# Graph network on one core: head projections of the first layer one round later, and another order of VectorE's products

## The reference

```
msg_s, msg_v = (projected node)[src] + (projected node)[dst]
m1_s, m1_v   = tensor product of msg with y, weighted by rbf @ W_rbf        # "M"
a            = leaky(m1_s @ W_alpha) . alpha_dot                            # logits, "alog"
val_s, val_v = m1_s @ Ws_val, m1_v @ Wv_val ; val_v *= sigmoid(val_s @ Wg)
m2_s, m2_v   = tensor product of (sigmoid(val_s), val_v) with y             # "M2"
h            = m2_s @ Ws_vlin, m2_v @ Wv_vlin                               # head values, "h_tab"
out          = node + (softmax over each destination of a, times h, summed) @ Wp
```

## Time and profile before

| what | value |
|---|---|
| median of three runs | 4853.46 us (4850.1 to 4861.61) |
| span of the profiled execution | 3828.1 us |
| own time of the profiled execution, beyond its span | not given |
| first layer's rounds | from 82 to 2226 us of the span |
| softmax, sums, node work | between the two |
| second layer's products (L1844) | from 2668 to 3766 us |
| TensorE / VectorE / ScalarE / GpSimd busy, of the span | 3407.1 / 3541.0 / 3089.1 / 2570.9 us |

### The profile page before, as it was taken

One profiled execution on the slowest core, in us unless ns is written; L12 is line 12 of the kernel. 1 busy time (PEld: TensorE's weight loads), 2 busy tenths in 40 slices (PEclk: granted clock), 3 DMA queues, 4 the chain that ended last, 5 costly groups with the idle time before them and its releaser, 6 DMA issues. The chain is left out here.

```text
span 3828.1 us, 96308 instructions
## 1 busy us (share of the span) xinstructions
PE 3407.1 (89%) x21340; PEld 2641.0 (69%) x21340; DVE 3541.0 (92%) x12738; ACT 3089.1 (81%) x11217; POOL 2570.9 (67%) x2469
## 2 busy tenths in 40 slices
PE   4899999999999999999999939976999999999997
PEld 3888888888888888888888838864333333333335
DVE  5999999999999999999999978874999999999995
ACT  4888899899989988988899847754787877778774
POOL 1777777777777777777777711111777777777772
PEclk8999999999999999999999979987999999999999
DMA  4333333333333333333333359971333433343333
GB/s 110 89 95 92 92 95 94 92 95 93 95 94 93 95 92 94 93 93 93 94 93 95 93 186 270 274 204 44 92 94 95 95 94 95 95 95 93 95 94 115
DMA packets 299642, 411.02 MB, mean 107 GB/s; under 512 B 98580, under 2 KB 234772, under 8 KB 299316
## 3 DMA queue, kind: packets, MB, share of 16 engines
q0 software_dynamic: 127008, 208.99, 24.2%
q1 hardware_dynamic: 172564, 201.26, 16.3%
HBM read 309.09 MB, written 100.94 MB: 107 GB/s over the span
## 5 line engine op out<-in xcount | busy, mean ns | idle before, releaser
L658 POOL DMA_INDIRECT SC<-dst_tab,idx x784 | 904.5, 1154 | 238.8 <-issue 237.3
L721 POOL DMA_INDIRECT ACC<-hid_tab,idx x784 | 811.4, 1035 | 348.6 <-issue 340.3
L658 POOL DMA_INDIRECT ACC<-src_tab,idx x784 | 758.5, 967 | 313.1 <-issue 164.2
L800 PE MATMUL TR<-ident,M 128*128 128x128 f32 x4704 | 664.4, 277 | 136.9 <-DVE M L1529 135.5
L800 PEld LDWEIGHTS TR<-ident,M 128*128 128x128 f32 x4704 | 520.1, 141 | 229.9 <-DVE M L1529 229.8
L1124 ACT ACTIVATE MT<-TR 128x768 f32<-128x768 f32 x784 | 596.9, 825 | 3.5 <-PE TR L800 3.5
L1113 ACT ACTIVATE ACC<-W,ACC 128x64 f32<-128x64 f32 x2352 | 577.7, 336 | 0.0
L849 PE MATMUL HP<-w_hv,MT 128*128 128x128 f32 x3136 | 520.2, 288 | 0.0
L824 PE MATMUL E<-w_mv,MT 128*128 128x128 f32 x3136 | 476.7, 275 | 0.0
L824 PEld LDWEIGHTS E<-w_mv,MT 128*128 128x128 f32 x3136 | 436.6, 191 | 0.0
L1306 ACT ACTIVATE ACC<-TR,y 128x128 f32<-128x128 f32 (+1 forms) x1568 | 417.2, 551 | 1.3 <-PE TR L982 1.2
(11 more groups left out here) (278 smaller groups left out, 7662.5 us busy)
## 6 DMA issues: line engine op xcount, KB each, us to landing
h_tab<-ACC SPq DMA_DIRECT2D x392, 160.0 KB
SC<-h_tab SPq DMA_DIRECT2D x50, 640.0 KB, 4.8
TAB<-h_tab SPq DMA_DIRECT2D x48, 640.0 KB, 5.2
ACC<-in_e64T SPq DMA_DIRECT2D x98, 256.0 KB
ACC<-src_tab,idx POOLq DMA_INDIRECT x784
SC<-dst_tab,idx POOLq DMA_INDIRECT x784
ACC<-hid_tab,idx POOLq DMA_INDIRECT x784, 3.4
agg_tab<-ACC POOLq DMA_DIRECT2D x49, 240.0 KB, 4.0
```

What stands on the lines that cost most here:

```text
L658: pool.indirect_dma_start(gat[:, v.slot8, g, :], None, table.ap(), bass.IndirectOffsetOnAxis(ap=idx[:, v.sslot, c + g:c + g + 1], axis=0))\
L721: pool.indirect_dma_start(gat1[:, v.slot8, g, :], None, hid_tab.ap(), bass.IndirectOffsetOnAxis(ap=idx[:, v.sslot, c:c + 1], axis=0))\
L800: ins = nc.tensor.transpose(to[:, b * G + g, :], Mt[:, g, lo:lo + w], ident[:, :])
```

## The change

TensorE's stage had e1(t-1), t2(t-2), t1(t), factors0(t+2), hm(t-2). It now has hm(t-3) between t2 and t1. MT2 gets a second buffer and ScalarE's copy into it waits for hm of two rounds before instead of one. `scalars0`, `head_products`, `head_values` and `store` move to round t-3, and the loops of those four engines end one stage later. GpSimd is as before.

VectorE's order becomes, by the old line numbers: 1540, 1478, 1546, 1503, 1554, 1509, 1557, 1567, 1581, 1603, 1583, 1584, 1585, 1591, 1593, 1612, 1514, 1515, 1521, 1522, 1528, 1529. For this `summed` is split into `summed` and `lifted`, `mixed` into `mixed_dots` and `mixed_crosses`, `mixed_sums` into `mixed_dot_sums` and `mixed_cross_sums`, and `sum_of_dots0` is taken out of `rest_of_s0`. Each function keeps the waits of its instructions, and `mixed_dots` has those of `mixed`.

```diff
+        MT2s = (MT2, sb("MT2b", [P, 3, G, P]))
 # SP
-                store(t + -2, total)
-            loop_steps(sp, Q, NS, False, 7, 2, sp0)
+                store(t + -3, total)
+            loop_steps(sp, Q, NS, False, 7, 3, sp0)
 # TensorE (hm reads MT2s[v.par] instead of MT2)
                 t2(t + -2, total)
+                hm(t + -3, total)
                 t1(t, total)
                 factors0(t + 2, total)
-                hm(t + -2, total)
-            loop_steps(pe, Q, NS, False, 2, 2, stage0)
+            loop_steps(pe, Q, NS, False, 2, 3, stage0)
 # ScalarE, copies
-                if v.past(1):
-                    act.wait_ge(LA[freed], v.num)
+                if v.past(back):
+                    act.wait_ge(LA[freed], v.num + 1 - back)
 ...
-                copies(t + -2, total, "t2", TR2, MT2, "c2", "h")
-                copies(t, total, "t1", TR1, MT, "c1", "e1")
+                copies(t + -2, total, "t2", TR2, MT2s[(t + -2).par], "c2", "h", 2)
+                copies(t, total, "t1", TR1, MT, "c1", "e1", 1)
 ...
-                scalars0(t + -2, total)
-            loop_steps(act, Q, NS, False, 2, 2, stage0)
+                scalars0(t + -3, total)
+            loop_steps(act, Q, NS, False, 2, 3, stage0)
 # VectorE, stage0
                 gated(t + -1, total)
                 added = messages(t + 1, total)
                 ups = gated_up(t + -1, total)
-                done = summed(t + -1, total, ups)
                 parts = products0(t + 1, total, added)
+                summed(t + -1, total)
+                crossed0(t + 1, total, parts)
+                done = lifted(t + -1, total, ups)
                 scaled(t + -1, total, done)
-                crossed0(t + 1, total, parts)
-                mixes = mixed(t + -1, total)
-                mixed_sums(t + -1, total, mixes)
-                up = head_products(t + -2, total)
+                dots = mixed_dots(t + -1, total)
+                up = head_products(t + -3, total)
+                crosses2 = mixed_crosses(t + -1, total)
+                mixed_dot_sums(t + -1, total, dots)
+                mixed_cross_sums(t + -1, total, crosses2)
+                head_values(t + -3, total, up)
                 crosses = others0(t + 1, total, parts)
-                head_values(t + -2, total, up)
+                sum_of_dots0(t + 1, total, parts)
                 rest_of_s0(t + 1, total, parts)
                 rest_of_v0(t + 1, total, parts, crosses)
-            loop_steps(dve, Q, NS, False, 1, 2, stage0)
+            loop_steps(dve, Q, NS, False, 1, 3, stage0)
```

More of the change, by code:

```diff
@@ L846, in hm @@
                 for g in range(G):
-                    nc.tensor.matmul(HP[:, S * g:S * (g + 1)], MT2[:, 0, g, :], w_hs0[:, :], start=True, stop=True)
+                    nc.tensor.matmul(HP[:, S * g:S * (g + 1)], MT2s[v.par][:, 0, g, :], w_hs0[:, :], start=True, stop=True)
                     for b in range(2):
-                        ins = nc.tensor.matmul(HP[:, P + P * g:P + P * (g + 1)], MT2[:, 1 + b, g, :], w_hv0[:, b, :],
+                        ins = nc.tensor.matmul(HP[:, P + P * g:P + P * (g + 1)], MT2s[v.par][:, 1 + b, g, :], w_hv0[:, b, :],
                                                start=(b == 0), stop=(b == 1))
@@ L1115, in weigh0, with copies @@
                     ins.then_inc(LA["ws"], 1)
-            def copies(v, total, turned, tr, dst, sem_done, freed):
+            def copies(v, total, turned, tr, dst, sem_done, freed, back):
                 if not inside(v, total):
@@ L1515, in others0, with sum_of_dots0 @@
                     return ch.count(TT(fX[:, :, 2], feat(S + 2 * C, (-2 * C, 2), (1, C)), wgt(192, (128, 2), (1, C)), ALU.mult))
-            def rest_of_s0(v, total, parts):
+            def sum_of_dots0(v, total, parts):
                 if parts:
@@ L1521, in rest_of_s0 @@
                     TT(mid(C, (1, C)), mid(0, (1, C)), mid(C, (1, C)), ALU.add)
+            def rest_of_s0(v, total, parts):
+                if parts:
+                    mid, feat, wgt, dots = parts
                     TT(mid(96, (S, 2), (1, S)), feat(0, (0, 2), (1, S)), wgt(C, (S, 2), (1, S)), ALU.mult)
@@ L1547, in gated_up, with summed @@
                                        ALU.mult))
-            def summed(v, total, up):
+            def summed(v, total):
                 if not inside(v, total):
@@ L1555, in summed, with lifted @@
                                                  ax(la[:, 0, 0:1], (LG, G * H), (1, LG)), AX.X, ALU.add))
+            def lifted(v, total, up):
+                if not inside(v, total):
+                    return
                 ch.wait(up)
@@ L1568, in scaled, with mixed_dots @@
                     .then_inc(LA["vg"], 1)
-            def mixed(v, total):
+            def mixed_dots(v, total):
                 if not inside(v, total):
@@ L1579, in vec, with mixed_crosses, mixed_dot_sums, mixed_cross_sums @@
                     return ax(V2[:, 0, C * k:C * k + 1], (96, G), *dims)
-                dots = ch.count(TT(ax(M2[:, v.par, 0, 0:1], (M0, G), (C, 3), (1, C)), vec(0, (C, 3), (1, C)),
+                return ch.count(TT(ax(M2[:, v.par, 0, 0:1], (M0, G), (C, 3), (1, C)), vec(0, (C, 3), (1, C)),
                                    y_of(v, 1, (1, 3), (0, C)), ALU.mult))
+            def mixed_crosses(v, total):
+                if not inside(v, total):
+                    return
+                def vec(k, *dims):
+                    return ax(V2[:, 0, C * k:C * k + 1], (96, G), *dims)
                 TT(fX2[:, :, 0:2, 0, :], vec(0, (C, 2), (1, C)), y_of(v, 2, (1, 2), (0, C)), ALU.mult)
                 TT(fX2[:, :, 0:2, 1, :], vec(1, (C, 2), (1, C)), y_of(v, 1, (1, 2), (0, C)), ALU.mult)
[L1585 to L1589, removed]
+                return ch.count(TT(fX2[:, :, 2], vec(2, (-2 * C, 2), (1, C)), y_of(v, 1, (2, 2), (0, C)), ALU.mult))
+            def mixed_dot_sums(v, total, dots):
+                if inside(v, total):
                     ch.wait(dots)
                     TT(M2[:, v.par, :, C:2 * C], M2[:, v.par, :, 0:C], M2[:, v.par, :, C:2 * C], ALU.add)
+            def mixed_cross_sums(v, total, crosses):
+                if inside(v, total):
                     ch.wait(crosses)
```

## The result

| comparison | kernel before | changed kernel | ratio, 95% interval |
|---|---|---|---|
| first, the one that was predicted | 4857.5 us | 5055.3 us (5039.3 to 5076.8) | 1.042 [1.039, 1.046] |
| second | 3818.8 us | 3946.1 us | 1.034 [1.032, 1.036] |
| third, on yet another chip | 3818.7 us | 3938.8 us | 1.031 [1.030, 1.033] |

The change makes the kernel slower in all three comparisons, by 198 us in the first comparison and by 127 and 120 us later. The forecast was +96 us and 4949 us, in a range up to 4990. The time is outside the range.

What follows compares the result with a forecast made beforehand. VectorE and GpSimd were taken to run at the same pace, 5.455 us a round. VectorE's 5.32 + 0.34 for pairs + 0.04 left of delays gave 5.70, +96 us over 390 rounds: 4949 us, range 4888 to 4990 (ends +41, +135).

Steps and rivals of the forecast that it cites:

- e1: TensorE's matmuls after ScalarE's copy of TR1; forecast to start 1.75 us after t1, ending near 4.0, over 1 us before `gated`.
- The base: Level the loss was added to: 5.455 us rounds from a 3828.1 us span, 1025 us around it unchanged.
- The pairs: VectorE's dependent neighbours: lifted to scaled (first) costs 0.22, scaled to mixed_dots (second) 0.12, together 0.34 us a round.
- The rule on the semaphore that costs nothing: Between two VectorE instructions the pipe empties anyway, so a semaphore adds nothing; by it the new neighbours would cost nothing.
- Spread reads: VectorE's PSUM reads spread over the round let GpSimd in more often; gain from nothing to 0.135 us a round.
- the 2.65 us issue: GpSimd gather issue stretched from 0.94 us, read as contention with VectorE's two-SBUF-input instructions, ending as VectorE reaches L1612.
- Head projections early, second MT2 buffer: TensorE loses 0.4 us before e1, 5.25 a round, still under 5.70; cost 0, from 0 to 0.05.
- A: Rival at L1557, L1567, L1581: stalls cost nothing and GpSimd gains; round 5.32, -53 us, 4801 us; chance 0.05.
- B: Rival: VectorE's stalls come out at half (0.17), all contention goes; round 5.49, +14 us, 4867 us; chance 0.06.
- D: Rival: GpSimd's issues stay stretched, late gathers stay; round 5.80, +135 us, 4988 us; held in the forecast's own range.
- C, the ring: Rival: loop of head projections, t1, ScalarE's copy and HP read grows from 5.4 to 5.9; +174 us, 5028; chance 0.08.

Runs made afterwards that it cites:

- without pairs: The changed kernel with one other instruction placed between lifted and scaled and between scaled and mixed_dots on VectorE: 3823.6 us, ratio 0.9989 to the kernel before.
- The heads alone: The changed kernel with VectorE's old order; head projections, values, scalars and store stay one round later, with second MT2 buffer: 3820.4 us, ratio 0.9985 to the kernel before.

## Why the prediction was wrong

*The base (failed).* The step was "I take what lies around the span as unchanged", with 1025 us around it. Those 1025 us were not around the span but inside it, in executions at another level. The sum of +96 us stands on rounds of 5.455 us in which VectorE's queue sets the pace, so that "nothing hides" a stall there and the way from TensorE to `gated` has more than 1 us to spare. In the runs that were timed neither held. The changed kernel's first layer took 3133 us there (L1479 from 86.3 to 3219.0), 8.0 us a round; with the 198 us taken off, the kernel before has about 7.5, an estimate, since it was never profiled at that level. VectorE was busy 857 of the 1200 us from 600 to 1800, against 1163 in the second comparison, and stood for E1 and HP:

```profile
600.00:1800.00 1200.00, 899.99 (x6001) 828.58 (x6000) 856.82 (x3306) 737.84 (x2701) 585.76 (x601) 0.89 0.22 64
...
L1545 DVE SCALAR_TENSOR_TENSOR la<-E,adot 128x144 f32<-128x144 f32 x392 | 120.2, 307 | 550.0 <-PE E L825 270.5
...
L1624 DVE TENSOR_TENSOR tG<-HP,ACC 128x192 f32<-128x192 f32 x392 | 138.9, 354 | 246.5 <-remote 188.0
```

A ratio instead of a time would have been nearer but not right either: the forecast was 1.025 (96 of 3828), 1.034 and 1.031 were measured at 3820 us, and 1.042 at 4857. Where the base fits, the loss of 127 and 120 us lies between the forecast's ends, 41 and 135.

*The pairs (right; the second, and what surrounds them, somewhat low).* Where the base fits, 5.76 us a round stand against the forecast 5.70. The first pair's mean spacing is 0.484 (forecast 0.49). The second's is 0.431 (0.39), with 0.45 as its median in the second comparison; in the third the mean is 0.419 and the median 0.39. One term was missing: L1504 stands 0.307 behind L1551, where 0.265 separated L1557 and L1503, so 0.04 more in every variant with the new order. Its four waits now have a single instruction before them after the gathered rows are added; that this is the reason was not tested. With 0.04 for this and 0.04 for the second pair the 5.70 become 5.78.

*The rule on the semaphore that costs nothing.* This is the one that the prediction takes from the Trainium skill ("VectorE: DVE Perf Modes", "The DRAIN you can't avoid"). The runs decide against it for this kernel, as the rows had: taking the pairs apart, with all semaphores kept, brings the time from 3946 to 3824 us and the ratio from 1.034 to 0.999.

*Spread reads (no gain of their own).* The late gathers went, as forecast, but no time with them: without pairs the round is 5.45 us as before. The reading of the 2.65 us issue was also too simple. It lasted over L1603, which reads PSUM as L1612 does. The other issues speak both ways. From 600 to 1800 us of the kernel before, 50 issues have their first 0.94 us beside instructions with two SBUF inputs alone, and 40 of them last over 1.2 us. In the changed kernel there are 106 such issues, all of 0.96 to 0.98 us, while the 52 issues over 1.2 us begin near the round's end and reach over L1545, which reads PSUM. So it is not shown that such instructions alone stretch an issue.

*Head projections early, second MT2 buffer (right at 3820 us).* The heads alone give 0.999. What I had not seen is that they are needed: without them the new VectorE order costs 7%.

*Rivals.* A and B fell with the pairs. D in its own form did not come: GpSimd waits for M. C, the ring, does not decide at 3820 us. In the first comparison the sign named for C is there, a round above 5.85 us with VectorE idle before `gated` and `head_products`. It can't be counted for C, since the kernel before has long rounds there too and nobody knows how much of that idle time it has.

*What stays open: the remaining part at 4850 us.* +198 us were measured, against +127 and +120 at 3820 us. In that profile VectorE's pairs are as elsewhere (means 0.483 and 0.410), so in us they cost no more than elsewhere, and less where VectorE would have waited anyway. Some 70 us at the least therefore come from something else. L1545 comes 1.69 us behind L1534 (0.27 in the second comparison) and L1624 0.88 behind L1591 on the mean, for want of E1 and HP. The trail leads to TensorE. A place in the timeline:

```profile
1023.14 0.82 PE L801 MATMUL TR<-ident,M 128*128 128x128 f32 x6
...
1027.26 0.81 ACT L1125 ACTIVATE MT<-TR 128x768 f32<-128x768 f32 x1 [3.85 <-remote]
...
1028.12 0.55 PE L823 MATMUL E<-w_ms,MT 128*128 128x168 f32 x2 [3.40 <-ACT MT L1125]
...
1029.89 0.31 DVE L1545 SCALAR_TENSOR_TENSOR la<-E,adot 128x144 f32<-128x144 f32 x1 [1.77 <-PE E L825]
```

The transposes are recorded as over at 1023.96, yet ScalarE gets to copy them only at 1027.26. "Remote" means that no recorded instruction ended near the update of the semaphore. The semaphore records say it in general: in this profile, from 900 to 1700 us, updates from the factors come at the median 1.9 us behind the recorded end, from t1 1.3, from the head projections 0.8, from e1 0.01 (but a third of e1's come late too); ScalarE's that release the other engines 0.01. In the changed kernel's profile at 3820 us TensorE's all come at 0.01. A matmul's recorded end is modelled, so the likeliest reading is that TensorE really finished late there. The granted clock does not explain it by itself. It was 0.89 over the stretch, where it was 1.00 in the second comparison. But from 600 to 3200 us, 103 rounds (counted from L1545 to L1545) had the full clock all through, and they took 8.27 us on the mean, not less than the 7.91 of the 220 rounds with a lowered clock in them. Behind t1 stand the copy and then e1, with only the factors beside them since the change, so it is plausible that the head projections' new place, free at 3820 us, costs something there. Neither that nor its contrary was shown, because no later run met this level.

## What to carry to other kernels

Before a time is added to a median, compare the span with it. Where they differ by more than a few us, the profile may be of other conditions. Then neither a time nor, as here, a ratio is sure to carry over, and the engine that set the pace in the profile need not set it in the runs. On an engine that is full, look in every new order for an instruction that directly follows the one it depends on, and price it from a place where the trace already shows the same two side by side, such as the last rounds of a loop. One unrelated instruction between them gave back here all that the change had lost at 3820 us. A read that is moved earlier needs its producer moved earlier in the same change.

## What the runs showed of the hardware

- The same program took 3819 to 3825 us (medians) on four chips and 4857 us in the first comparison, with the same number of instructions and nearly the same durations on VectorE (351 against 355 ns for L1869). TensorE's semaphore updates were not the same (at the median 1.3 us late after t1 and 1.9 after the factors, against 0.01), nor the granted clock (0.892 to 0.895 over the changed kernel's runs, against 0.974 to 0.975). Which of these is cause and which effect is open.
- A VectorE instruction of 192 elements that waits for the one ahead starts 0.39 to 0.45 us after it, and 0.48 where two other waits stand before that wait; 0.27 without. That the number of waits makes the 0.48 was not tested.
- An indirect DMA issue on GpSimd takes 0.94 us and the next one begins 0.30 us behind it; single issues lasted 2.65 us in the kernel before and 1.6 in the changed one. Spreading VectorE's PSUM reads moved the long issues and left the sum: 933 us in 1200 before and after (and 510.8 + 422.1 in the kernel without pairs).
